# Loading sixteen tiles of y instead of four ahead of pass 2 of a two-layer convolution kernel

## The chip, the cores and the metric

The kernel runs on one core of one Trainium2 chip. The metric is the device time of one execution in microseconds. Engines: PE (TensorE), ACT (ScalarE), DVE (VectorE), POOL (GpSimd), and SP (SyncE), which here only issues DMAs. SPq marks SP's DMA issues in the rows.

## What is computed

x is 2048 x 512 channels x 8 x 8, float32. Two layers, each with a residual:

```python
x = x + L0(_gn(x))     # an 8x8 Clifford algebra product on each channel's 64 elements, plus a bias
x = x + L1(_gn(x))     # _gn: group norm of 32 groups of 16 channels
# L1(v):
h = sign(batchnorm(v, bn1))                        # statistics over batch and pixels
h = conv3x3(h, sign(conv_w) * scale, groups=16)
h = batchnorm(h, bn2) + v
return where(h > 0, h, prelu_a * h)
```

The two batch norms need statistics over the whole batch, so the work falls into three passes. Between them y (the input of L1, the normalised output of layer 0) and h (the sums of the convolution, packed as integers) go through DRAM.

## The kernel before, in words

**Pass 1** has B = 128 units of 16 images. SP loads a unit of x (2 MB) into one of the four slots of ring_x; ACT takes means and squares with ring_g as scratch (x_mean, x_square, lines 563 to 576); PE turns the unit into psT and ACT copies it to ring_gT (561); PE multiplies (product, 1024 to 1033; semaphore mixed); DVE evicts psV into ring_z (756, evicted) and counts it (765, z_counted); POOL normalises ring_z into ring_y (467, y_done); SP stores a unit of y (341). The very last unit's y is written by ACT (614, y_last) and stored by SP (370). Every x, z and y ring is therefore free at another moment.

**Between the passes** DVE, PE and POOL work out the coefficients of the first batch norm, bn1_c, in a chain of small instructions.

**Pass 2** has T2 = 256 tiles: 32 images by 128 channels, one tile for each pair of units and quarter of the channels. Tile t takes units 2(t // 4) and the next, so tiles 0 to 15 read units 0 to 7 only. For each tile:
- SP loads y in two halves of 512 KB (load_y2, 359) into slot t % 4, two slots to a unit's slot of ring_x (slots 0 and 1 of it).
- ACT takes the sign of both halves (take_sign, 624; semaphore signed) into a slot in ring_x's last quarter.
- DVE packs both into one frame (840; packed). PE runs 18 matmuls on it (1100; conv_done) into one of four PSUM regions.
- ACT converts the sums to words (unpack, 635) in word slot t % 4. It waits for PE, and from tile 4 on for the store of the word tile four before (h_stored) and its statistics (h_counted). ACT's order is: sign of t, then unpack of t - 2.
- DVE takes statistics of the words (848). SP stores them (store_h, 378), 512 KB.

All DMAs of the kernel are issued by SP in program order. In pass 2, SP's round t is: wait for the sign of t, load tile t + 4, store words t - 3. Before the rounds SP does, in this order: the store of unit 125 (in pass 1's last round), tiles 0 to 3 of y, the store of unit 126, the wait for y_last, the store of unit 127, and a wait until all of y is stored.

**Pass 3** reads y and h again (load_3, 395 and 397) and writes the output (rings y, z, g and gT hold its inputs). It begins with loads that SP puts between the last three stores of h. The change does not touch it.

Of the kernel before, what the change touches and what calls it, by code (L numbers as in the profile page):

```python
# [18 lines left out]
SIDE = 8  # L19
J = C // P  # L20
NQ = 4
# [3 lines left out]
FU = NQ * SL  # L25
UNIT = NQ * (P // GROUPS)
BANK = 512
PAIRS = GC // 2
HEAD = TAIL = 4
SLOTS = 4  # L30
# [4 lines left out]
IMG = 16  # L35
# [21 lines left out]
def two_layer_kernel(nc, x, w0, b0, conv_w, g1, be1, g2, be2, prelu_a, ident_in, quarter_in, clif_in, pick_in, route_in, out):  # L57
    N = x.shape[0]
    B = N // UNIT
    T2 = (B // 2) * J  # L60
# [15 lines left out]
    with ExitStack() as ctx:  # L76
# [3 lines left out]
        def sem(name):  # L80
            return ctx.enter_context(nc.semaphore(name))

        ring_x = sb("ring_x", [P, SLOTS, FU])
        ring_z = sb("ring_z", [P, 2, FU])
# [91 lines left out]
        def y2_slot(s):  # L176
            return ring_x[:, s // 2, 2048 * (s % 2):2048 * (s % 2) + 2048]

        def word_slot(s):
            return ring_x[:, 2, 1024 * s:1024 * s + 1024].bitcast(I32)  # L180

# [68 lines left out]
        bn1_routed = sem("bn1_routed")  # L250

        y2_loaded = [sem(f"y2_loaded{s}") for s in range(SLOTS)]
        signed = sem("signed")
        packed = sem("packed")
        conv_done = sem("conv_done")
# [25 lines left out]
        def rounds(eng, body, total, head=HEAD):  # L281

            loops = (total - head - TAIL) // SLOTS
            for c in range(head):
                body(0, c)
            with eng.Fori(0, loops) as i:
                for c in range(head, head + SLOTS):
                    body(i, c)
            for c in range(head, head + TAIL):
                body(loops, c)  # L290

        def from_round(i, c, n):

            return not (isinstance(i, int) and SLOTS * i + c < n)
# [5 lines left out]
        def row(ap, b):  # L300
            if isinstance(b, int):
                return ap[b]
            one = ap[bass.ds(b, 1)]
            return one.rearrange("a p f -> (a p) f") if len(one.shape) == 3 else one.rearrange(
                "a p n f -> (a p) n f")
# [7 lines left out]
        @block.sync  # L313
        def _(sp):
            def load_x(i, c):
                s = c % SLOTS
                sp.dma_start(ring_x[:, s, :].rearrange("p (n f) -> p n f", n=NQ), row(xb, SLOTS * i + c)).then_inc(
                    x_loaded[s], 16)

            load_x(0, 0)  # L320
            for dst, src in ((ident[:, :], ident_in), (quarter[:, :], quarter_in), (clif, clif_in),
                             (pick[:, :], pick_in), (route[:, :], route_in),
                             (cw, conv_w.rearrange("(k p) i a b -> p k (i a b)", p=P)),
                             (gb1[:, 0, :], g1.rearrange("(k p) -> p k", p=P)),
                             (gb1[:, 1, :], be1.rearrange("(k p) -> p k", p=P)),
                             (gb2[:, 0, :], g2.rearrange("(k p) -> p k", p=P)),
                             (gb2[:, 1, :], be2.rearrange("(k p) -> p k", p=P)),
                             (w0_sb[:, :], w0.rearrange("o i p -> (i p) o"))):
                sp.dma_start(dst, src, allow_slow_non_contiguous=True).then_inc(const_loaded, 16)
            sp.wait_ge(cleared, 1)  # L330
            sp.dma_start(brow[0:1, :], b0.rearrange("(a o) k -> a (o k)", a=1)).then_inc(const_loaded, 16)
            load_x(0, 1)
            for m in range(4):
                sp.dma_start(slope[GROUPS * m:GROUPS * (m + 1), :],
                             prelu_a.rearrange("(q j) -> q j", j=GC)).then_inc(const_loaded, 16)
            load_x(0, 2)

            def store_y(i, c):
                b = SLOTS * i + c
                sp.wait_ge(y_done, 4 * b + 4)  # L340
                sp.dma_start(row(y_unit, b), ring_y[:, c % 2, :]).then_inc(y_stored[c % 2], 16)

            def pass1(i, c):
                b = SLOTS * i + c
                if until(i, c, B - 3):
                    if from_round(i, c, 1):
                        sp.wait_ge(evicted, 4 * b)
                    load_x(i, c + 3)
                if from_round(i, c, 2):
                    store_y(i, c - 2)  # L350

            rounds(sp, pass1, B)

            def load_y2(i, c):

                s = c % SLOTS
                pair = 2 * (i + c // J)
                for e in range(2):
                    sp.dma_start(y2_slot(s)[:, 1024 * e:1024 * (e + 1)].rearrange("p (m f) -> p m f", m=4),  # L359
                                 row(y_chan[:, c % J], pair + e)).then_inc(y2_loaded[s], 16)  # L360

            sp.wait_ge(evicted, 4 * (B - 2))
            sp.wait_ge(y_stored[0], 16)
            sp.wait_ge(y_stored[1], 16)
            for c in range(SLOTS):
                load_y2(0, c)
            loops1 = (B - SLOTS) // SLOTS
            store_y(loops1, SLOTS - 2)
            sp.wait_ge(y_last, NQ)
            sp.dma_start(y_unit[B - 1], ring_y[:, 1, :]).then_inc(y_stored[1], 16)  # L370

            for s in range(2):
                sp.wait_ge(y_stored[s], 16 * (B // 2))

            def store_h(i, c):
                t = SLOTS * i + c
                sp.wait_ge(unpacked, t + 1)
                sp.dma_start(row(h_chan[:, c % J], i + c // J),  # L378
                             word_slot(c % SLOTS).rearrange("p (m f) -> p m f", m=4)).then_inc(h_stored[c % SLOTS], 16)

            def pass2(i, c):
                t = SLOTS * i + c
                if until(i, c, T2 - SLOTS):
                    sp.wait_ge(signed, 2 * t + 2)
                    load_y2(i, c + SLOTS)
                if from_round(i, c, 3):
                    store_h(i, c - 3)

            rounds(sp, pass2, T2, 2 * HEAD)

            def load_3(i, c):

                s = c % SLOTS
                for e in range(2):
                    sp.dma_start(y3_slot(s)[:, e].rearrange("p c f -> p (c f)"),
                                 row(y_half[:, c % 2], SLOTS * i + c // 2 * 2 + e)).then_inc(y3_loaded[s], 16)
                sp.dma_start(h3_slot(s), row(h_half[:, c % 2], 2 * i + c // 2)).then_inc(h3_loaded[s], 16)

            for s in range(SLOTS):
                sp.wait_ge(h_stored[s], 32)  # L400
            loops2 = (T2 - SLOTS) // SLOTS
            for c in range(1, SLOTS):
                store_h(loops2, c)
                load_3(0, c - 1)
            load_3(0, SLOTS - 1)
            for s in range(SLOTS):
                sp.wait_ge(h_stored[s], 16 * (T2 // SLOTS))

            def store_out(i, c):
                half = c % 2  # L410
                for e in range(2):
                    sp.dma_start(row(ob, SLOTS * i + c // 2 * 2 + e)[:, :, 512 * half:512 * half + 512],
                                 o_slot(half)[:, e]).then_inc(out_stored[half], 16)

            def pass3(i, c):
                t = SLOTS * i + c
                if from_round(i, c, 1):
                    sp.wait_ge(added, 8 * t)
                    if until(i, c, T3 - 3):
                        load_3(i, c + 3)  # L420
                    store_out(i, c - 1)

            rounds(sp, pass3, T3)
            sp.wait_ge(added, 8 * T3)
            store_out((T3 - SLOTS) // SLOTS, SLOTS - 1)
            for s in range(2):
                sp.wait_ge(out_stored[s], 16 * T3)
# [115 lines left out]
        def _(act):  # L543
# [73 lines left out]

            def take_sign(i, c):
                t, s = SLOTS * i + c, c % SLOTS
                act.wait_ge(y2_loaded[s], 32 * (i + c // SLOTS + 1))  # L620
                if from_round(i, c, 2):
                    act.wait_ge(packed, t - 1)
                for e in range(2):
                    act.activation(  # L624
                        sign_slot(c % 2)[:, e].rearrange("p (a n b) -> p n a b", a=SIDE, n=IMG),
                        y2_slot(s)[:, 1024 * e:1024 * (e + 1)].rearrange("p (n a b) -> p n a b", n=IMG, a=SIDE),
                        ACT.Sign, bias=bn1_c[:, c % J, 1:2], scale=bn1_c[:, c % J, 0:1]).then_inc(signed, 1)

            def unpack(i, c):
# [13 lines left out]
                if from_round(i, c, 2):  # L643
                    unpack(i, c - 2)

            rounds(act, pass2, T2, 2 * HEAD)
            last = (T2 - SLOTS) // SLOTS
            unpack(last, SLOTS - 2)
            unpack(last, SLOTS - 1)
# [519 lines left out]
```

## Time and profile before

| | |
|---|---|
| Median of 3 runs | 4575.77 us (4575.63 to 4576.2) |
| The profiled execution | 4573.96 us, span 4572.2 us |
| Mean granted TensorE clock in it | 0.993 |
| Busy: PE, DVE, ACT, POOL | 93%, 91%, 85%, 32% of the span |
| DMA | 1612 MB, mean 353 GB/s |
| Pass 1, between, pass 2, pass 3 | to about 1748, 1761, 2795, 4572 us |

Times in rows are microseconds from the span's start. A timeline row is start, duration, engine, line, operation, output<-inputs, shapes and count; in brackets the engine's idle time before it and what ended it. A row with a count above 1 is several instructions, merged. The duration of a DMA issue is SP's time for issuing it, not that of the transfer. PEclk is the granted TensorE clock as a share of full speed. The DMA share is the mean busy share of the core's 16 DMA engines; the profile counts it a little generously, so it can stand above 1.

### The profile page before, as it was taken

The page shows a single profiled execution, that of the slowest core. Times are in us where ns is not written, and L with a number is a line of the kernel's source. Part 1 is how long each engine was busy: PE and PEld are TensorE (multiplying, and loading weights), DVE is VectorE, ACT ScalarE, POOL GpSimd, SP SyncE. Part 2 cuts the span into 40 slices and gives each one's busy share as a digit, 9 for nine tenths or more (in the row PEclk, how much of TensorE's full clock was granted, in tenths as well). Part 3 has the DMA queues.
Part 4 walks back from the last instruction along what each step waited for, and adds up shares of the span by engine and source line. Part 5 has one row for each costly group of instructions (what it writes and reads, how often), then busy time and mean ns, then how long its engine had stood idle before and what let it go on. Part 6 is the DMA issues. An engine that isn't in the chain of part 4 may idle for free.

```text
span 4572.2 us, 82027 instructions
## 1 busy us (share of the span) xinstructions
PE 4262.5 (93%) x21700; PEld 2705.5 (59%) x21956; DVE 4171.5 (91%) x9974; ACT 3866.0 (85%) x5521; POOL 1470.4 (32%) x3476
## 2 busy tenths in 40 slices
PE   6999999999999998999999996999999999999998
PEld 6999999999999994444444443444444444444443
DVE  5999999999999998999999998999999999999998
ACT  7999999999999996888888886777777777777776
POOL 3888888888888883000000000000000000000000
PEclk9999999999999998999999998999999999999999
DMA  5888888888888889999999998999999999999998
GB/s 189 317 321 317 317 320 317 317 321 316 317 321 317 316 312 330 385 385 385 385 385 385 385 385 325 386 390 386 390 384 390 388 386 386 389 389 387 388 387 308
DMA packets 686039, 1612.17 MB, mean 353 GB/s; under 512 B 29811, under 2 KB 423795, under 8 KB 620467
## 3 DMA queue, kind: packets, MB, share of 16 engines
q1 hardware_dynamic: 686002, 1611.74, 96.0%
q8 instruction: 16, 0.26, 0.0%
q14 instruction: 21, 0.16, 0.0%
HBM read 940.55 MB, written 671.09 MB: 352 GB/s over the span
## 4 chain that ended last, share of the span: by engine, by line
PE 50%; SPq 20%; ACT 11%; DVE 9%; issue 9%; DMA 1%; DVEq 0%; ACTq 0%; POOL 0%
PE psV L1032 17%; SPq L359 12%; PE psT L1015 10%; DVE ring_x L971 8%; SPq L378 7%; PE psT L1123 5%; PE psT L1125 5%; PE psV L1125 4%; PE psV L1123 4%; PE psV L1029 3%; ACT ring_y L670 3%; ACT ring_z L670 3%; ACT ring_g L568 2%; PE psV L1119 1%; ACT late L660 1%
## 5 line engine op out<-in xcount | busy, mean ns | idle before, releaser
L1032 PE MATMUL psV<-W0T,ring_gT 128*128 128x128 f32 x8192 | 1080.4, 275 | 47.7 <-issue 34.0
L1032 PEld LDWEIGHTS psV<-W0T,ring_gT 128*128 128x128 f32 x8192 | 1077.1, 192 | 33.7
L765 DVE BATCH_NORM_STATS2 early<-ring_z 128x6 f32<-128x128 f32 x4096 | 822.6, 274 | 0.0
L756 DVE SCALAR_TENSOR_TENSOR ring_z<-psV,x_r,ring_x 128x1024 f32<-128x1024 f32 x512 | 657.3, 1284 | 118.5 <-DVE early L765 76.7
L660 ACT ACTIVATE late<-ring_x,minus_b 128x512 f32<-128x512 f32 x1024 | 639.4, 707 | 0.9 <-PE psV L1125 0.9
L848 DVE BATCH_NORM_STATS2 h_tup<-ring_x 128x6 f32<-128x512 uint16 x1024 | 630.9, 679 | 0.5
L467 POOL TENSOR_SCALAR ring_y<-ring_z,u_r,u_nm 128x1024 f32<-128x1024 f32 x508 | 601.1, 1199 | 35.6 <-POOL gn L486 35.6
L624 ACT ACTIVATE ring_x<-ring_x,bn_c 128x1024 f16<-128x1024 f32 x512 | 604.1, 1230 | 5.3 <-DVE bn_c L831 5.3
L574 ACT ACTIVATE ring_g<-ring_x,x_ms 128x1024 f32<-128x1024 f32 x512 | 585.2, 1143 | 0.0
L561 ACT ACTIVATE ring_gT<-psT 128x1024 f32<-128x1024 f32 x512 | 523.8, 1023 | 50.3 <-PE psT L1015 24.6
L1015 PE MATMUL psT<-ident,ring_x 128*128 128x128 f32 x4096 | 540.2, 275 | 4.0 <-ACT rank_lhs L580 0.4
L1100 PE MATMUL psT<-late 128*128 128x448 f16 (+3 forms) x2304 | 479.5, 363 | 62.1 <-DVE late L840 61.9
L670 ACT ACTIVATE ring_y<-ring_y,gnb 128x512 f32<-128x512 f32 x512 | 368.0, 801 | 200.0 <-DVE ring_x L971 175.8
L568 ACT ACTIVATE ring_g<-ring_x 128x1024 f32<-128x1024 f32 x512 | 536.9, 1049 | 0.0
L670 ACT ACTIVATE ring_z<-ring_z,gnb 128x512 f32<-128x512 f32 x512 | 368.1, 801 | 190.3 <-DVE ring_x L971 190.3
L1125 PE MATMUL psT<-late,early 128*128 128x512 f32 x1024 | 523.7, 593 | 0.0
L1100 PE MATMUL psV<-late 128*128 128x448 f16 (+3 forms) x2304 | 475.5, 362 | 30.9 <-DVE late L840 30.9
L989 DVE SCALAR_TENSOR_TENSOR ring_x<-ring_x,bn_q,psV 128x512 f32<-128x512 f32 x512 | 374.6, 745 | 117.7 <-PE psV L1125 90.6
L1015 PEld LDWEIGHTS psT<-ident,ring_x 128*128 128x128 f32 x4096 | 460.2, 141 | 26.4 <-ACT rank_lhs L580 26.3
L1100 PEld LDWEIGHTS psT<-late 128*128 128x128 f16 x2304 | 215.9, 98 | 324.9 <-issue 75.9
L840 DVE SCALAR_TENSOR_TENSOR late<-ring_x 128x1024 f16<-128x1024 f16 x256 | 312.8, 1222 | 97.9 <-ACT ring_x L624 89.2
L1125 PE MATMUL psV<-late,early 128*128 128x512 f32 x768 | 392.1, 592 | 0.0
(161 smaller groups left out, 5591.5 us busy)
## 6 DMA issues: line engine op xcount, KB each, us to landing
ring_x<-in_x SPq DMA_DIRECT2D x128, 2048.0 KB, 8.8
y_scratch<-ring_y SPq DMA_DIRECT2D x128, 2048.0 KB, 12.7
ring_x<-y_scratch SPq DMA_DIRECT2D x512, 512.0 KB, 7.6
out<-ring_x SPq DMA_DIRECT2D x256, 1024.0 KB, 14.5
h_scratch<-ring_x SPq DMA_DIRECT2D x256, 512.0 KB, 7.8
ring_y<-y_scratch SPq DMA_DIRECT2D x128, 1024.0 KB, 7.9
ring_z<-y_scratch SPq DMA_DIRECT2D x128, 1024.0 KB, 8.3
ring_g<-h_scratch SPq DMA_DIRECT2D x64, 1024.0 KB, 12.1
```

The costliest lines, as they stand in the source:

```text
L467: pool.tensor_scalar(ring_y[:, c % 2, :].rearrange("p (r n s) -> p n r s", r=GC, n=NQ)[:, j], ring_z[:, c % 2, SL * j:SL * (j + 1)].rearra ...
L568: act.activation(ring_g[:, 2 * (j % 2), :], ring_x[:, s, SL * j:SL * (j + 1)], ACT.Copy, scale=-1.0 / (SL * ROOT), accum_out=x_ms[:, s, 0, ...
L624: act.activation(sign_slot(c % 2)[:, e].rearrange("p (a n b) -> p n a b", a=SIDE, n=IMG), y2_slot(s)[:, 1024 * e:1024 * (e + 1)].rearrange ...
L660: act.activation(relu_slot(m), t_slot(c % 2)[:, m], ACT.Relu, bias=minus_b2[:, ch:ch + 1], scale=-1.0).then_inc(relu_done, 1)
L670: last = act.activation(v, v, ACT.Identity, bias=gnb[:, s, e, 0, n:n + 1], scale=gnb[:, s, e, 1, n:n + 1])
L756: dve.scalar_tensor_tensor(out=ring_z[:, c % 2, cols], in0=psV[:, j % 2, :], scalar=x_r[:, s, j:j + 1], in1=ring_x[:, s, cols], op0=ALU.mu ...
L765: last = dve.bn_stats(z_tup[:, s, j, 2 * r:2 * r + 2, :].rearrange("p h t -> p (h t)"), ring_z[:, c % 2, SL * j + 2 * S * r:SL * j + 2 * S ...
L848: last = dve.bn_stats(h_tup[:, c % J, c // J, q, :], parts[:, BANK * q:BANK * (q + 1)])
L1015: last = pe.transpose(psT[:, j % 2, P * r:P * (r + 1)], ring_x[:, s, SL * j + P * r:SL * j + P * (r + 1)], ident[:, :])
L1032: last = pe.matmul(psV[:, j % 2, P * r:P * (r + 1)], ring_gT[:, j, P * r:P * (r + 1)], W0T[:, :], start=False, stop=(r % 4 == 3))
L1100: last = pe.matmul(sums[:, IMG * a.start:IMG * a.stop, b.start:b.stop], conv_wT[:, c % J, tap, :], rows[:, IMG * (a.start + dy):IMG * (a.s ...
L1125: pe.matmul(sum_bank(m), diag[:, 8 * (c % 2) + m, :], relu_slot(m), start=False, stop=True).then_inc(combined, 1)
```

## The change

Tiles 4 to 15 of y get places of their own, and semaphores of their own (y2_early): tiles 4 and 5 in ring_g, 6 and 7 in ring_gT, 8 to 11 in ring_z, 12 to 15 in ring_y. SP issues their loads before pass 2's rounds, each group behind a wait for the last user of its ring. In rounds 0 to 3 SP loads tiles 16 to 19 into the slots of ring_x, in rounds 4 to 15 nothing, and from round 16 on tile t + 4 as before. The rounds of SP and ACT are unrolled for 16 tiles instead of 8.

```diff
--- before.py
+++ after.py
@@ -25,6 +25,7 @@
 FU = NQ * SL
 UNIT = NQ * (P // GROUPS)
 BANK = 512
+AHEAD = 16
 PAIRS = GC // 2
 HEAD = TAIL = 4
 SLOTS = 4
@@ -176,6 +177,16 @@
         def y2_slot(s):
             return ring_x[:, s // 2, 2048 * (s % 2):2048 * (s % 2) + 2048]
 
+        def y2_place(i, c):
+
+            if not (isinstance(i, int) and SLOTS <= SLOTS * i + c < AHEAD):
+                return y2_slot(c % SLOTS)
+            n = SLOTS * i + c - SLOTS
+            if n < SLOTS:
+                return (ring_g if n < 2 else ring_gT)[:, 2 * (n % 2):2 * (n % 2) + 2, :].rearrange("p s f -> p (s f)")
+            return (ring_z if n < 2 * SLOTS else ring_y)[:, :, :].rearrange("p s f -> p (s f)")[
+                :, 2048 * (n % SLOTS):2048 * (n % SLOTS) + 2048]
+
         def word_slot(s):
             return ring_x[:, 2, 1024 * s:1024 * s + 1024].bitcast(I32)
 
@@ -250,6 +261,7 @@
         bn1_routed = sem("bn1_routed")
 
         y2_loaded = [sem(f"y2_loaded{s}") for s in range(SLOTS)]
+        y2_early = [sem(f"y2_early{t}") for t in range(SLOTS, AHEAD)]
         signed = sem("signed")
         packed = sem("packed")
         conv_done = sem("conv_done")
@@ -353,24 +365,36 @@
 
             def load_y2(i, c):
 
-                s = c % SLOTS
+                early = isinstance(i, int) and SLOTS <= SLOTS * i + c < AHEAD
+                loaded = y2_early[SLOTS * i + c - SLOTS] if early else y2_loaded[c % SLOTS]
                 pair = 2 * (i + c // J)
                 for e in range(2):
-                    sp.dma_start(y2_slot(s)[:, 1024 * e:1024 * (e + 1)].rearrange("p (m f) -> p m f", m=4),
-                                 row(y_chan[:, c % J], pair + e)).then_inc(y2_loaded[s], 16)
+                    sp.dma_start(y2_place(i, c)[:, 1024 * e:1024 * (e + 1)].rearrange("p (m f) -> p m f", m=4),
+                                 row(y_chan[:, c % J], pair + e)).then_inc(loaded, 16)
 
             sp.wait_ge(evicted, 4 * (B - 2))
-            sp.wait_ge(y_stored[0], 16)
-            sp.wait_ge(y_stored[1], 16)
+            for s in range(2):
+                sp.wait_ge(y_stored[s], 16 * (AHEAD // J))
             for c in range(SLOTS):
                 load_y2(0, c)
             loops1 = (B - SLOTS) // SLOTS
+            sp.wait_ge(x_squared, NQ * B)
+            load_y2(1, 0)
+            load_y2(1, 1)
+            sp.wait_ge(mixed, NQ * B)
+            load_y2(1, 2)
+            load_y2(1, 3)
             store_y(loops1, SLOTS - 2)
             sp.wait_ge(y_last, NQ)
             sp.dma_start(y_unit[B - 1], ring_y[:, 1, :]).then_inc(y_stored[1], 16)
+            sp.wait_ge(z_counted, NQ * B)
+            for c in range(SLOTS):
+                load_y2(2, c)
 
             for s in range(2):
                 sp.wait_ge(y_stored[s], 16 * (B // 2))
+            for c in range(SLOTS):
+                load_y2(3, c)
 
             def store_h(i, c):
                 t = SLOTS * i + c
@@ -381,12 +405,16 @@
             def pass2(i, c):
                 t = SLOTS * i + c
                 if until(i, c, T2 - SLOTS):
-                    sp.wait_ge(signed, 2 * t + 2)
-                    load_y2(i, c + SLOTS)
+                    if not from_round(i, c, SLOTS):
+                        sp.wait_ge(signed, 2 * t + 2)
+                        load_y2(i, c + AHEAD)
+                    elif from_round(i, c, AHEAD):
+                        sp.wait_ge(signed, 2 * t + 2)
+                        load_y2(i, c + SLOTS)
                 if from_round(i, c, 3):
                     store_h(i, c - 3)
 
-            rounds(sp, pass2, T2, 2 * HEAD)
+            rounds(sp, pass2, T2, AHEAD)
 
             def load_3(i, c):
 
@@ -617,13 +645,18 @@
 
             def take_sign(i, c):
                 t, s = SLOTS * i + c, c % SLOTS
-                act.wait_ge(y2_loaded[s], 32 * (i + c // SLOTS + 1))
+                if not from_round(i, c, SLOTS):
+                    act.wait_ge(y2_loaded[s], 32)
+                elif not from_round(i, c, AHEAD):
+                    act.wait_ge(y2_early[t - SLOTS], 32)
+                else:
+                    act.wait_ge(y2_loaded[s], 32 * (i + c // SLOTS + 2 - AHEAD // SLOTS))
                 if from_round(i, c, 2):
                     act.wait_ge(packed, t - 1)
                 for e in range(2):
                     act.activation(
                         sign_slot(c % 2)[:, e].rearrange("p (a n b) -> p n a b", a=SIDE, n=IMG),
-                        y2_slot(s)[:, 1024 * e:1024 * (e + 1)].rearrange("p (n a b) -> p n a b", n=IMG, a=SIDE),
+                        y2_place(i, c)[:, 1024 * e:1024 * (e + 1)].rearrange("p (n a b) -> p n a b", n=IMG, a=SIDE),
                         ACT.Sign, bias=bn1_c[:, c % J, 1:2], scale=bn1_c[:, c % J, 0:1]).then_inc(signed, 1)
 
             def unpack(i, c):
@@ -643,7 +676,7 @@
                 if from_round(i, c, 2):
                     unpack(i, c - 2)
 
-            rounds(act, pass2, T2, 2 * HEAD)
+            rounds(act, pass2, T2, AHEAD)
             last = (T2 - SLOTS) // SLOTS
             unpack(last, SLOTS - 2)
             unpack(last, SLOTS - 1)
```

## Rows read from the trace of the kernel before

**Rows 1.** The page: span, then DMA share and GB/s in 40 slices.
```profile
span 4572.2 us, 82027 instructions
...
DMA  5888888888888889999999998999999999999998
GB/s 189 317 321 317 317 320 317 317 321 316 317 321 317 316 312 330 385 385 385 385 385 385 385 385 325 386 390 386 390 384 390 388 386 386 389 389 387 388 387 308
```

**Rows 2.** Table by stage: window, its length, each engine's busy time, PEclk, DMA share, GB/s.
```profile
0.00:1748.00 1748.00, 1640.66 (x13240) 1546.65 (x13496) 1594.99 (x5168) 1659.07 (x2702) 1455.01 (x3454) 1.00 0.85 308
1748.00:1761.00 13.00, 2.50 (x9) 2.13 (x10) 5.04 (x21) 7.69 (x8) 7.17 (x13) 0.50 0.80 335
1761.00:2795.00 1034.00, 947.23 (x4590) 431.90 (x4588) 938.38 (x1398) 833.70 (x763) 7.15 (x10) 1.00 1.09 384
```

**Rows 3.** Groups of instructions, 1900 to 2700 us: busy, mean ns, idle before and releasers.
```profile
L624 ACT ACTIVATE ring_x<-ring_x,bn_c 128x1024 f16<-128x1024 f32 x392 | 462.7, 1230 | 0.0
...
L635 ACT ACTIVATE ring_x<-psT 128x1024 int32<-128x1024 f32 x98 | 100.3, 1023 | 79.1 <-DMA h_scratch<-ring_x 73.1 <-DVE h_tup L848 6.0
```

**Rows 4.** Timeline of SP's queue, 1729 to 1755 us.
```profile
1729.60 0.33 SPq L341 DMA_DIRECT2D y_scratch<-ring_y  x1
1730.05 12.31 SPq L359 DMA_DIRECT2D ring_x<-y_scratch  x8
1742.41 1.87 SPq L341 DMA_DIRECT2D y_scratch<-ring_y  x1
1751.69 0.36 SPq L370 DMA_DIRECT2D y_scratch<-ring_y  x1
```

**Rows 5.** Timelines of ACT, PE and DVE: their last work of pass 1 on each ring.
```profile
1714.44 1.14 ACT L574 ACTIVATE ring_g<-ring_x,x_ms 128x1024 f32<-128x1024 f32 x1
...
1736.06 1.05 PE L1032 MATMUL psV<-W0T,ring_gT 128*128 128x128 f32 x8
...
1741.01 3.16 DVE L765 BATCH_NORM_STATS2 early<-ring_z 128x6 f32<-128x128 f32 x16
```

**Rows 6.** Table of shorter windows, columns as in rows 2.
```profile
1738.00:1748.00 10.00, 0.00 (x0) 0.00 (x0) 6.73 (x28) 0.97 (x1) 9.17 (x23) 0.58 1.10 353
1749.00:1757.00 8.00, 2.25 (x8) 2.00 (x8) 3.82 (x20) 2.69 (x4) 2.25 (x5) 0.50 1.01 434
1758.40:1761.60 3.20, 0.86 (x3) 0.43 (x4) 1.23 (x1) 3.20 (x4) 3.20 (x5) 0.50 0.17 46
```

**Rows 7.** Timeline of the first tiles of pass 2, 1759 to 1784 us.
```profile
1759.59 10.44 SPq L359 DMA_DIRECT2D ring_x<-y_scratch  x8
...
1760.74 8.59 PE L1100 MATMUL psT<-late 128*128 128x512 f16 x36 [5.96 <-DVE late L840]
...
1769.17 7.30 PE L1100 MATMUL psV<-late 128*128 128x512 f16 x36
...
1770.07 0.51 SPq L378 DMA_DIRECT2D h_scratch<-ring_x  x1
...
1776.31 7.30 PE L1100 MATMUL psT<-late 128*128 128x512 f16 x36
...
1780.08 1.02 ACT L635 ACTIVATE ring_x<-psT 128x1024 int32<-128x1024 f32 x1 [0.29 <-PE psT L1100]
```

**Rows 8.** Timeline of SP's queue at the load of tile 20.
```profile
1820.64 2.40 SPq L359 DMA_DIRECT2D ring_x<-y_scratch  x2
```

**Rows 9.** Landing times of lines 378 and 359; timeline at pass 2's end.
```profile
DMA to landing us min/median/max: 3.2/7.8/17.4
...
DMA to landing us min/median/max: 3.9/7.6/10.8
...
2798.37 1.06 SPq L395 DMA_DIRECT2D ring_y<-y_scratch  x2
...
2800.31 1.23 SPq L378 DMA_DIRECT2D h_scratch<-ring_x  x1
...
2817.81 0.17 DVE L958 TENSOR_SCALAR gnb<-gn 128x16 f32<-128x16 f32 x1 [2.12 <-DMA h_scratch<-ring_x]
```

## The prediction

> **What bounds the kernel now.** I read the page first, for the shape of the whole run [rows 1]: the core's 16 DMA engines show hardly any slack from slice 17 on, and some before it. A table by stage puts numbers on that [rows 2]. Pass 1 ends about 1748 and moves 308 GB/s at a DMA share of 0.85, so engines set its pace. Pass 2 moves 384 GB/s at a share of 1.09 for 1034 us, which is a full DMA system. The groups of instructions of 800 us of pass 2 show the same from the engines' side [rows 3]: 392 Sign activations, two for each tile, so 196 tiles in 800 us, 4.08 us a tile. ACT's idle time before the conversion of the sums to words (L635) was ended by the store of h, in all but 6 of 79 us in the group shown. A tile moves two halves of y, 1.049 MB, and one word tile, 0.524 MB; 1.573 MB at 385 GB/s is 4.09 us. So **pass 2 is bound by bytes**. Without that bound a tile would take 3.57 us: in the first tiles PE runs 36 matmuls, two tiles, in 7.14 us (1776.31 less 1769.17, one group's start to the next) [rows 7].
>
> Then I read SP's queue at the boundary [rows 4]. SP issues the store of unit 125 at 1729.60, tiles 0 to 3 of y behind it, the store of unit 126 at 1742.41 and that of unit 127 at 1751.69; tiles 4 to 7 begin at 1759.59 and the first store of h follows at 1770.07 [rows 7]. The windows show what the DMA does in between [rows 6]: loads of y alone go at 353 GB/s and stores of y alone at 434, both with a share above 1. Only 1758.4 to 1761.6 is nearly idle. **The end of pass 1, from 1729.6 on, has almost no free DMA time.**
>
> **The change, part by part.** (1) *Tiles 4 to 7 go into ring_g and ring_gT.* Their waits are for ACT's last square, which ends at 1716, and PE's last product, which ends about 1737; both are over when SP gets there, at 1742.4 [rows 4, 5]. So the waits cost nothing, but the eight DMAs stand in front of the store of unit 126. Nobody needs that store early: ACT's y of unit 127 waits for unit 125's.
> (2) *Tiles 8 to 11 go into ring_z* behind unit 127's store; the wait, for the last statistics (over by 1744.2 [rows 5]), is free. *Tiles 12 to 15 go into ring_y* once both y stores have landed. Eight DMAs are queued behind unit 127 by then, so the queue does not run dry.
> (3) *Tiles 16 to 19* are issued in rounds 0 to 3 of SP's pass 2, where tiles 4 to 7 were, in front of the first store of h. Rounds 4 to 15 issue stores of h alone. From round 16 on the order is as before: a load four tiles ahead, and a store three behind.
> (4) The twelve semaphores, and Sign reading other rings of the same type and shape, I cost at nothing; the instruction is the same 1.2 us one and no engine gains one.
>
> The chief cost is in what is queued ahead of the first store of h. It was four tiles; now twelve more (4.2 MB of tiles 4 to 7 before the y stores, 8.4 MB of tiles 8 to 15 after) come first. I follow the queue in its order of issue.
> - Unit 125 and tiles 0 to 3 are 6.3 MB and are through at 1748: in the before trace the 353 GB/s stretch of loads ends there [rows 6].
> - Tiles 4 to 7, 4.19 MB at 353 GB/s: 11.9 us, to 1759.9.
> - Units 126 and 127, 4.19 MB at 434 GB/s: 9.7 us, to 1769.6.
> - Tiles 8 to 19, 12.58 MB at 353 GB/s: 35.6 us, to 1805.2.
> - The first store of h, 0.52 MB, 1.2 us and about 1.5 us for the completion to arrive (its least landing time is 3.2 us, of which 1.2 are data [rows 9]): **landed at about 1808**. If the loads went at pass 2's 385 GB/s throughout, it would be 4 us sooner, at 1804.
>
> Who waits for it: ACT converts tile 4 into word slot 0, and for that the store of tile 0 must have landed. Before, that instruction began at 1780.08 with PE as its releaser [rows 7]. It will now wait until 1808, **28 us** (24 by the faster rate). Queued behind it on ACT are the Signs of tile 7 and later; DVE packs nothing without them and PE convolves nothing without the pack. All three stand still, and PE's granted clock will fall to 0.50, as it did in the gap between the passes [rows 6].
>
> What comes back: after 1808 tiles 4 to 19 are in the SBUF, and the engines go at 3.57 us a tile. But the DMA has only stores of h until the Sign of tile 16 lets SP issue tile 20. Sign of tile 7 begins at 1809; nine rounds of 3.57 are 32.1; Sign itself is 2.4; the slow clock costs 1.4 (two tiles took 8.59 us for 7.14 at the start [rows 7]), and about 2 come back because PE has emptied its queue of two tiles and starts tile 7 sooner after ACT. Sum 1842.9. Issue (0.9) and a landing on an almost empty queue (3.9, the least of the line that loads [rows 9]) put **tile 20 in the SBUF at 1847.7**. Before, its two halves were issued from 1820.64 on, the second at 1821.9 [rows 8], and landed the median 7.6 us later [rows 9], at 1829.5. From tile 20 on both kernels issue the same transfers in the same order and have 4.09 us of DMA work for each tile of 3.57 us, so both are bound by bytes and the distance stays: 18.2 us. I add 1 us for the start of the stream (1761.6, the restart before, came 2 us after its issue). **Sum: +19 us**, and +15 by the faster rate of loads.
>
> A count of idle DMA time agrees. After: 1807 to 1843 holds only the stores of tiles 4 to 12 or so, ten times 1.2 to 1.4 us, so 23 us are idle; before, 3 us at 1758.4 and about 2 more in the restart were. The difference is 18.
>
> The profiled execution took 4573.96 us, 1.8 under the median of 4575.77. Its sum is 4593; on the median **4595 us**. Against before, 0.2%, 9 us, is about what a measurement of this kernel can tell from no change.
>
> **A rule weighed.** The last store of h of pass 2, issued at 2800.31 behind loads for pass 3, took the longest of all to land, 17.4 us, and DVE waited for it until 2817.81 [rows 9]: transfers of SP land in the order in which their data is queued. The Trainium skill, DMA: Bandwidth & Descriptors, Queues, rings and completion order, says that on each DMA engine descriptors of one issuer's ring are consumed in ring order; by it the same 28 us stall follows. The same page's Rules for kernel authors advise to issue a DMA early and to wait for it late; by that rule alone the sum would be rival A's, since it counts the covered latency and not who stands behind the load.
>
> **Rivals.**
> *A, not slower: the stores of h pass the loads.* If a store of h shares the engines with the loads queued before it rather than following them, it lands in some 8 us like the median one, ACT never stops, and tiles 4 to 15 run at 3.57 instead of 4.08 us: 12 times 0.51 is 6.1 us, 4569.7 us. It decides where the landing stays below the 10 us between the store's issue and ACT's need (1770.07 to 1780.08 [rows 7]). For it: nothing but the early start of the loads. Against: 17.4 us above, and the bytes, as the DMA would still be full from 1742 on and could save only the 5 us in which it was idle.
> *B, a short stall.* The loads go faster than 353, or PE and ACT make up more after the stall, as ACT alone needs 3.38 us a tile. For each us that the DMA is idle less, one comes back. With half of it, +9 us: 4585 us. Against: PE's 3.57.
> *C, a longer one.* The loads of y slow the two y stores, the wait for unit 127 leaves a gap, or the stores of tiles 1 to 3 are late one after the other and each stops ACT again: 5 to 8 us more, 4602 us. Against: these stores follow each other at 1.2 us, ACT needs one each 3.57.
> *D, the loads are not early.* Twelve tiles are not loaded "while the first pass ends": SP's place in line lets only tiles 4 to 7 start before 1748. That is in my sum already; if SP sat still in front of them as well, the time would be C's.
>
> **How the numbers follow.** Forecast 0.80, A 0.07, B 0.07, C and D 0.06. The forecast's own range, with both rates of loads and 2 us either way, is 4589 to 4598. Nothing in A reaches 9 us of gain, so faster gets little, 0.03; within 0.2%, A's rest and half of B, 0.10; slower 0.87. The range is 4586 to 4602; it leaves out A, the lower part of B and the far end of C.
>
> **What would show it.** Right: one idle stretch of ACT of 24 to 30 us before a conversion (L635's new line) at 1780, released by the DMA of h_scratch; in the chain of waits it is the longest one; PE's clock at half in it; the first store of h issued near 1800 instead of 1770; after about 1808 a stretch of some 35 us with a low DMA share and a round each 3.6 us; then 385 GB/s again and pass 2's end some 19 us later. Pass 3's length unchanged. Wrong: no long wait for h_scratch, a first store of h that lands within 10 us, or a pass 2 that ends before 2795.

## The result and the profile after

The changed kernel takes 4595.66 us (median of 6 runs, 4594.82 to 4597.21) against 4575.70 for the kernel before (6 runs, 4574.46 to 4576.65): 20 us slower, ratio 1.0044 with a 95% interval of 1.0031 to 1.0057. The forecast was 4595.

The page of the changed kernel, span, DMA share and GB/s in 40 slices, answers to [rows 1]:

```profile
span 4594.9 us, 81949 instructions
...
DMA  5888888888888888999999998999999999999998
GB/s 189 317 324 315 317 319 319 316 316 323 313 319 321 317 304 293 360 385 385 385 385 385 385 385 324 386 386 388 388 387 385 390 387 389 387 388 387 390 384 310
```

Slices 16 and 17 moved 293 and 360 GB/s where 330 and 385 stood before, although transfers now start sooner. The other slices changed by a few GB/s at most. SP's queue at the boundary, with the columns of [rows 4], says in which order it now works:

```profile
1729.43 0.33 SPq L353 DMA_DIRECT2D y_scratch<-ring_y  x1
1729.88 12.31 SPq L372 DMA_DIRECT2D ring_x<-y_scratch  x8
1742.24 6.20 SPq L372 DMA_DIRECT2D ring_g<-y_scratch  x4
1748.48 5.71 SPq L372 DMA_DIRECT2D ring_gT<-y_scratch  x4
1754.23 1.87 SPq L353 DMA_DIRECT2D y_scratch<-ring_y  x1
1756.15 0.43 SPq L389 DMA_DIRECT2D y_scratch<-ring_y  x1
1756.62 19.83 SPq L372 DMA_DIRECT2D ring_z<-y_scratch  x8
1776.55 11.94 SPq L372 DMA_DIRECT2D ring_y<-y_scratch  x8
1788.54 12.16 SPq L372 DMA_DIRECT2D ring_x<-y_scratch  x8
1800.74 37.75 SPq L402 DMA_DIRECT2D h_scratch<-ring_x  x13
1844.12 0.99 SPq L372 DMA_DIRECT2D ring_x<-y_scratch  x2
```

The first store of h is issued at 1800.74; before, it was at 1770.07 [rows 7]. SP goes through 24 issues of loads, one after the other, in 44 us. It issues them at the speed of the transfers: the eight for ring_y take 11.94 us, which for 4.19 MB is 351 GB/s, while with little in flight an issue takes 0.4 us (tile 20, at 1844.12). So most of the delay of the first store of h is a late issue. From its issue to its landing it took this long:

```profile
DMA to landing us min/median/max: 8.3/8.3/8.3
```

That is 1809.0; before, it was issued 30.7 us sooner and took 6.4. The last load in front of it, issued at 1799.28, landed 8.5 us later, at 1807.8, just ahead of it. ACT's timeline from 1778 us:

```profile
1777.74 1.02 ACT L668 ACTIVATE ring_x<-psV 128x1024 int32<-128x1024 f32 x1 [0.29 <-PE psV L1133]
1778.66 2.36 ACT L657 ACTIVATE ring_x<-ring_gT,bn_c 128x1024 f16<-128x1024 f32 x2
1809.14 1.02 ACT L668 ACTIVATE ring_x<-psT 128x1024 int32<-128x1024 f32 x1 [28.12 <-issue]
1810.07 2.36 ACT L657 ACTIVATE ring_x<-ring_gT,bn_c 128x1024 f16<-128x1024 f32 x2
...
1841.56 2.36 ACT L657 ACTIVATE ring_x<-ring_x,bn_c 128x1024 f16<-128x1024 f32 x2
```

There is the 28 us stall, before the conversion of tile 4. The profile puts the wait down to "issue" and not to the store, so that the releaser alone would mislead here. The time at which the store landed, 1809.0, and the code name it: h_stored is the one wait of this instruction that was not long satisfied. The table of windows of the changed kernel, columns as in [rows 2]:

```profile
1780.00:1790.00 10.00, 8.41 (x43) 3.99 (x41) 4.98 (x8) 1.02 (x1) 0.00 (x0) 1.00 1.10 349
1790.00:1800.00 10.00, 0.00 (x0) 0.00 (x0) 0.00 (x0) 0.00 (x0) 0.00 (x0) 0.67 1.10 349
1800.00:1810.00 10.00, 0.00 (x0) 0.00 (x0) 0.00 (x0) 0.86 (x1) 0.00 (x0) 0.50 1.10 363
...
1812.00:1843.00 31.00, 29.26 (x139) 14.05 (x140) 30.54 (x43) 28.81 (x28) 0.00 (x0) 0.92 0.44 147
...
1900.00:2700.00 800.00, 728.84 (x3528) 330.81 (x3527) 727.74 (x1089) 642.85 (x589) 0.00 (x0) 1.00 1.09 385
```

Read from the top: the DMA is full of loads, then all engines stand still behind them, then the engines run and the DMA is more than half idle, since it has only the stores of tiles 4 to 12 to carry. After that pass 2 is what it was. SP issues the first load of pass 3 at 2817.36 us; before, it was 2795.58. Nearly the whole loss lies between 1780 and 1850 us, where the second half of tile 20 lands (1844.71 and 5.2 us, against 1821.49 and 8.0 us before: 20.4 us later).

### The profile page after: what moved, and what is told of

It is laid out like the page before. It is cut to its first block, busy times and chain, and to the rows that moved or that the text cites. A ratio compares the mean times of both kernels' runs of the same rounds, so it can differ in the third digit from the quotient of the medians.

```text
span 4594.9 us, 81949 instructions
## 1 busy us (share of the span) xinstructions
PE 4264.2 (93%) x21700; PEld 2707.0 (59%) x21956; DVE 4171.1 (91%) x9974; ACT 3866.6 (84%) x5521; POOL 1470.8 (32%) x3476
## 4 chain that ended last, share of the span: by engine, by line
PE 32%; SPq 20%; DVE 14%; issue 12%; POOL 10%; ACT 9%; DMA 1%; DVEq 1%; POOLq 0%; ACTq 0%
SPq L372 13%; DVE ring_x L1004 8%; PE psV L1065 7%; SPq L402 6%; PE psT L1156 5%; PE psT L1158 5%; PE psT L1048 4%; PE psV L1158 4%; PE psV L1156 4%; POOL ring_y L495 3%; ACT ring_y L703 3%; DVE early L798 3%; ACT ring_z L703 3%; PE psV L1062 1%; DVE ring_z L789 1%
## 5 line engine op out<-in xcount | busy, mean ns | idle before, releaser
L657 ACT ACTIVATE ring_x<-ring_x,bn_c 128x1024 f16<-128x1024 f32 x488 | 575.9, 1230 | 5.3 <-DVE bn_c L864 5.3
L1133 PEld LDWEIGHTS psV<-late 128*128 128x128 f16 x2304 | 218.5, 98 | 309.7 <-issue 63.9
```

What stands on the lines that cost most here:

```text
L1133: last = pe.matmul(sums[:, IMG * a.start:IMG * a.stop, b.start:b.stop], conv_wT[:, c % J, tap, :], rows[:, IMG * (a.start + dy):IMG * (a.s ...
```

## The experiments

The theory is: pass 2 ends when its bytes are through, and the change leaves the DMA idle because the first stores of h stand in SP's queue behind all the loads, so that ACT stops. Rivals were a fixed cost of the change (other rings to read from, more unrolled code), a cost for each tile ahead wherever it stands, the delay of the stores of y, and the bytes in flight as such.

**Fewer tiles ahead.** The change with 8 and with 12 in place of 16; the groups of loads ahead of the rounds that this makes needless are gone.

```diff
-AHEAD = 16
+AHEAD = 8
```

> Only tiles 4 to 7 are loaded ahead. Queue theory (the first store of h waits for all that SP queued before it): in front of it stand, from 1748 on, 4.2 MB of tiles 4 to 7, 4.2 MB of y and 4.2 MB of tiles 8 to 11, so it lands about 1784 and ACT stands still for some 4 us before its conversion for tile 4; against the kernel before -1 to +2 us, about 4576. Rival (a fixed cost of the change, from reading y out of other rings, more semaphores or longer unrolled code): most of the 20 us is still there, 4590 or more. Rival (every tile ahead costs the same 1.7 us): +7 us, 4583.

> Tiles 4 to 11 are loaded ahead. Queue theory: one more group of four tiles (11.9 us) in front of the first store of h than with 8, it lands about 1796, ACT stands still 16 us, and tile 16 is loaded 8 to 9 us later than before: 4584 to 4585. Rival (a fixed cost): 4590 or more. Rival (the same for each tile): +13 us, 4589.

Measured 4578.75 us with 8 (ratio 1.0008, 0.9998 to 1.0017) and 4586.08 with 12 (1.0023, 1.0013 to 1.0032), the kernel before beside them at 4575.48. ACT's conversion of tile 4, first with 8 tiles ahead, then with 12:

```profile
1786.55 1.02 ACT L663 ACTIVATE ring_x<-psT 128x1024 int32<-128x1024 f32 x1 [6.64 <-issue]
```

```profile
1796.56 1.02 ACT L666 ACTIVATE ring_x<-psT 128x1024 int32<-128x1024 f32 x1 [15.75 <-issue]
```

The stall grows 6.6, 15.8, 28.1 us, the time 3, 11, 20; the 3 us alone are not clear of no change. A fixed cost is out. With 12 the queue's count held, 16 us of stall for 16; with 8 it was 2.6 us too low. Both times came about 1 us above what was expected. The windows with 8 tiles ahead show why:

```profile
1755.00:1768.00 13.00, 8.47 (x30) 3.63 (x31) 4.30 (x6) 8.97 (x9) 11.11 (x16) 0.62 1.06 409
1768.00:1775.00 7.00, 7.00 (x37) 3.47 (x36) 5.44 (x8) 6.42 (x7) 0.00 (x0) 1.00 0.53 188
1775.00:1786.00 11.00, 11.00 (x57) 5.38 (x55) 8.88 (x13) 4.63 (x5) 0.00 (x0) 1.00 1.10 354
```

SP waits for all of y to be stored, with nothing queued behind unit 127's store, and the DMA runs dry at 1768 to 1775: at a share of 0.53 against 1.06 it lost about half of 7 us. In the change, and with 12, eight loads stand behind that store and cover the wait (with 12, 361 GB/s at 1768 to 1775). The count by tiles also misses: 7 and 13 us were expected by it, and 3 and 11 came.

**Where the loads stand.** All sixteen tiles ahead, but the loads of tiles 16 to 19 moved behind the first stores of h:

```diff
-                    if not from_round(i, c, SLOTS):
-                        sp.wait_ge(signed, 2 * t + 2)
-                        load_y2(i, c + AHEAD)
-                    elif from_round(i, c, AHEAD):
+                    if from_round(i, c, AHEAD):
                         sp.wait_ge(signed, 2 * t + 2)
                         load_y2(i, c + SLOTS)
+                    elif from_round(i, c, 8) and not from_round(i, c, 12):
+                        sp.wait_ge(signed, 2 * t + 2)
+                        load_y2(i, c + 8)
```

> All sixteen tiles are loaded as in the change, but tiles 16 to 19 are issued in SP's rounds 8 to 11 and not in rounds 0 to 3, so that they stand behind the first stores of h. Queue theory: the first store of h lands 12 us sooner, about 1797, the idle time of ACT is 16 us in place of 28, and the time is 12 us less than the change's, about 4584. Rival (the number of tiles ahead of pass 2, or the rings they lie in, costs the time, wherever the stores stand): no change, 4596.

Measured 4584.36 us (1.0019, 1.0009 to 1.0028), 11.3 less than the change, and the conversion of tile 4:

```profile
1795.86 1.02 ACT L668 ACTIVATE ring_x<-psT 128x1024 int32<-128x1024 f32 x1 [16.36 <-issue]
```

The same tiles in the same rings: only the loads of four tiles changed their place in the order. That rules out the number of tiles and the rings as the cause of these 11 us. The 9 us that are left over the kernel before go with the 16 us of stall that are left.

**The stores of y first.** The change, with the loads of tiles 4 to 7 moved behind the stores of units 126 and 127:

```diff
-            sp.wait_ge(x_squared, NQ * B)
-            load_y2(1, 0)
...
-            load_y2(1, 3)
             store_y(loops1, SLOTS - 2)
             sp.wait_ge(y_last, NQ)
             sp.dma_start(y_unit[B - 1], ring_y[:, 1, :]).then_inc(y_stored[1], 16)
+            sp.wait_ge(x_squared, NQ * B)
+            load_y2(1, 0)
...
+            load_y2(1, 3)
```

> The change, but the stores of units 126 and 127 are issued before the loads of tiles 4 to 7. Queue theory: the same bytes stand before the first store of h, in another order, so it lands at 1807 to 1810 as in the change, ACT stands still 27 to 29 us, and the time is 4595 to 4597. Rival (what costs is that two stores of y are held back by loads, and with them the wait for all of y): most of the loss goes, 4585 or less.

Measured 4597.41 us (1.0047, 1.0032 to 1.0063), with ACT idle for 28.51 us before the conversion of tile 4, at 1810.41. Here the order among what stands before the store of h made no difference clear of the noise; delayed stores of y were not the cost.

**The stores of h on another queue.** The change with every load in its place; POOL, which has nothing to do in pass 2 after its first few us [rows 2], issues the first sixteen stores of h, with semaphores of their own:

```diff
-                if from_round(i, c, 3):
+                if from_round(i, c, AHEAD + 3):
                     store_h(i, c - 3)
...
+            for c in range(AHEAD):
+                pool.wait_ge(unpacked, c + 1)
+                pool.dma_start(row(h_chan[:, c % J], c // J),
+                               word_slot(c % SLOTS).rearrange("p (m f) -> p m f", m=4)).then_inc(h_soft[c % SLOTS], 16)
```

> The change with its loads where they are, but the first sixteen stores of h are issued by POOL, on its own queue. Queue theory in the strong form (it is the place in SP's queue that holds the stores back, not the bytes in flight): the stores share the DMA engines with the loads, land in 10 us or little more, ACT stands still for under 5 us, tile 16 is signed at engine pace at about 1815 and the time is 0 to 9 us under the kernel before, 4567 to 4576. Rival (the stores are held back by the bytes in flight, whichever queue they are on): ACT stands still until about 1805, and the time is that of the change, 4596.

Measured **4570.64 us** (0.9991, 0.9981 to 1.0000; before 4575.48): 25 us less than the change, from nothing but who issues sixteen stores. The interval ends at no change, but each of the 10 runs is faster than each of the 31 of the kernel before. Its DMA issues from 1755 to 1830 us, with size and median time from issue to landing:

```profile
q1 hardware_dynamic: 16759, 20.56, 77.4%
q0 software_dynamic: 2304, 8.39, 28.7%
...
h_scratch<-ring_x POOLq DMA_DIRECT2D x16, 512.0 KB, 6.6
ring_x<-y_scratch SPq DMA_DIRECT2D x16, 512.0 KB, 11.5
ring_z<-y_scratch SPq DMA_DIRECT2D x8, 512.0 KB, 13.1
ring_y<-y_scratch SPq DMA_DIRECT2D x8, 512.0 KB, 12.3
```

and ACT's conversion of tile 4, which waits for PE again as in [rows 7]:

```profile
1779.91 1.02 ACT L676 ACTIVATE ring_x<-psT 128x1024 int32<-128x1024 f32 x1 [0.29 <-PE psT L1141]
```

The DMA stays full:

```profile
1780.00:1800.00 20.00, 20.00 (x103) 9.82 (x102) 20.00 (x29) 18.56 (x18) 4.51 (x6) 1.00 1.07 384
1800.00:1820.00 20.00, 20.00 (x103) 9.98 (x102) 19.98 (x29) 18.27 (x17) 3.76 (x5) 1.00 1.06 385
```

The stores land in 6.6 us while the loads now take 11 to 13. So what held the stores was their place in SP's order, not the bytes in flight. Most of it is the time of issue: POOL issued its first store at 1766.97, 34 us before SP came to it in the change, and the landing after it differs by less than 2 us (8.3 against a median of 6.6). The Trainium skill, DMA: Bandwidth & Descriptors, Queues, rings and completion order, has each DMA engine take turns among the queues that have work for it; the landing times, 6.6 against 11 to 13 us, agree. The same page of the Trainium skill, Issuing engines are not separate DMA queues, says that issuing from several engines only saves the sequencer's time of issue. That holds here: the bandwidth is the same, 384 to 385 GB/s from 1780 to 1820 us, and what POOL saved is the wait for SP's turn. That section of the Trainium skill calls the time usually small beside the DMA itself; here it is 34 us for the first store, since a row of loads, each issued at the speed of the transfers, stands in front of it, and the kernel is 25 us faster without it.

**One load beside each store.** The same places, and SP alone; tiles 8 to 19 are loaded in rounds 2 to 13, and the wait for all of y moves to round 6.

```diff
-            for c in range(SLOTS):
-                load_y2(2, c)
...
+                    elif 2 <= t < 14:
+                        sp.wait_ge(signed, 2 * t + 2)
...
+                        load_y2(i, c + 6)
```

> The same sixteen places, tiles 4 to 7 queued ahead as in the change, but tiles 8 to 19 one in each of SP's rounds 2 to 13 (round t loads tile t + 6), each beside one store of h; the wait for all of y moves to round 6. Queue theory: the first store of h has two tiles and the y stores in front of it and lands at 1777 to 1780, so ACT does not stand still; the DMA has no gap at 1758 to 1763, which is worth 3 to 5 us: 4571 to 4573. Rival (loading ahead costs by its number of tiles or its rings): 4590 or more.

Measured 4572.09 us (0.9992, 0.9983 to 1.0001; before 4575.84). Its windows:

```profile
1758.40:1761.60 3.20, 1.52 (x5) 0.72 (x6) 1.86 (x2) 3.20 (x4) 3.20 (x5) 0.50 1.15 439
1761.60:1811.00 49.40, 49.40 (x242) 23.80 (x240) 41.44 (x58) 40.98 (x38) 5.05 (x8) 0.96 1.07 385
1811.00:1820.00 9.00, 8.99 (x45) 4.11 (x43) 7.96 (x11) 6.81 (x7) 0.00 (x0) 1.00 1.09 385
1820.00:1830.00 10.00, 9.31 (x46) 4.42 (x47) 9.61 (x15) 10.00 (x10) 0.00 (x0) 1.00 0.95 310
```

The idle 3.2 us of [rows 6] are filled, after tile 0 no wait of ACT up to 1815 us reaches 1 us, and the gain is 3.7 us, within the 3 to 5 that were expected. The interval just reaches no change, but each of the 11 runs is faster than each of the 21 of the kernel before. At 1820 to 1830, 310 GB/s, a little DMA time is lost again.

**The idle time of pass 1 as well.** As the last, with tiles 0 to 3 issued before the store of unit 125, three tiles behind the last store of y, and a lead of nine. In the kernel before, the DMA stands still here, since SP waits for POOL's y of unit 125 and no load is queued in front of that wait:

```profile
1724.50:1729.50 5.00, 4.95 (x44) 4.89 (x44) 4.96 (x18) 1.51 (x2) 4.76 (x5) 1.00 0.00 0
```

```diff
+                if isinstance(i, int) and b == B - 1:
...
+                    for n in range(SLOTS):
+                        load_y2(0, n)
                 if from_round(i, c, 2):
                     store_y(i, c - 2)
...
+                        load_y2(i, c + 9)
```

> As the kernel with a lead of 6, and tiles 0 to 3 are issued before the store of unit 125, at about 1717, into the DMA's idle time of 1723.5 to 1729.6; tiles 8 to 10 follow the last store of y and rounds 2 to 10 load tile t + 9. Queue theory: 6 us more of idle DMA time are used, the first store of h lands at about 1777, and pass 2 keeps to the engines' 3.57 us a tile up to tile 16: 6 to 9 us under before, 4567 to 4570. Rival (bytes before the first store of h are too many after all): a stall of ACT at tile 4 and a time at or over 4576.

Measured 4570.54 us (0.9989, 0.9980 to 0.9998; before 4575.84). The gain is 5.3 us, a little under what was expected. The windows at tiles 11 to 18 show where it went:

```profile
1800.00:1811.00 11.00, 11.00 (x57) 5.43 (x56) 9.96 (x15) 9.16 (x9) 0.00 (x0) 1.00 1.07 379
1811.00:1819.00 8.00, 7.83 (x40) 3.67 (x39) 7.39 (x12) 8.00 (x9) 0.00 (x0) 1.00 0.37 125
```

The DMA has run out of places to load to: all of tiles up to 19 are in, and by the program tile 20 may only come after the Sign of tile 16. SP issued it at 1818.22.

**Both.** The early tiles 0 to 3, all sixteen tiles ahead, and the first sixteen stores of h on POOL's queue.

> All sixteen tiles ahead as in the change, the first sixteen stores of h on POOL's queue, and tiles 0 to 3 issued before the store of unit 125, into the DMA's idle 6 us at 1723.5 to 1729.6. Theory (pass 2 ends when the bytes are through, as long as no store of h is kept from landing): the DMA is full from about 1722 to the end of pass 2, and the 6 us show on top of the run with POOL's stores alone: 4564 to 4566. Rival (that run has already reached what the engines allow at 3.57 us a tile, so earlier bytes find no taker): 4570 to 4571, with a stretch of low DMA share before tile 20 is issued.

Measured **4567.49 us** (0.9982, 0.9973 to 0.9991; before 4575.74), the fastest of all, 8 us under the kernel before and 28 under the change. It is 3.2 us below the run with POOL's stores alone, which was measured in another session (3.4 if each is set against the kernel before beside it), between the 5 to 6 that were expected and the rival's nothing. Its windows have both:

```profile
1748.00:1800.00 52.00, 41.27 (x191) 20.59 (x192) 36.21 (x64) 40.49 (x38) 20.74 (x32) 0.82 1.07 384
...
1811.00:1819.00 8.00, 8.00 (x42) 3.92 (x40) 8.00 (x12) 7.42 (x8) 1.53 (x3) 1.00 0.63 214
```

The engines go at their own pace, and still the DMA waits some 3 us (0.4 of 8) for the Sign of tile 16. SP issued tile 20 at 1817.39, as that Sign ended. This points to the Sign of tile 16 as the next limit with sixteen places; a version with more places was not tried.

## Why the prediction was right

Point by point, by its own steps:

- *Pass 2 is bound by bytes.* Shown: every run moves 385 GB/s at a share of 1.09 from 1900 to 2700 us, and the runs without a stall are faster than the kernel before by no more than the DMA's idle time that they filled.
- *Parts 1 to 3, the waits.* They cost nothing, as said: SP passed them at 1742.24, 1748.48 and 1756.62 without a pause. That the wait for all of y was covered by the eight loads behind it was right and mattered: with 8 tiles ahead that cover was gone, and half of 7 us with it.
- *The count of the queue.* It put the landing at 1808, or 1804 by the rate of 385 GB/s. It came at 1809.0, and ACT's conversion began at 1809.14. The slower rate was the right one: loads alone went at 349 GB/s at 1748 to 1760 and at 1780 to 1800 (353 taken).
- *The stall.* 28 us forecast, 28.12 measured; PE ran dry at about 1788 and its granted clock fell to 0.50 (1800 to 1810).
- *What comes back.* Sign of tile 7 at 1810.07 (1809), that of tile 16 ended at 1843.9 (1842.9), tile 20 issued at 1844.12. The slow clock cost PE 1.9 us, not 1.4: tile 7's 18 matmuls took 5.44 us against 3.57. The landing of tile 20 was counted too low: its second half came at 1849.9, not at 1847.7, so that the distance was 20.4 us there and not 18.2. The 1.2 us of a later issue and 1 us of a longer landing make it up. The reading of [rows 8] was off too, the second half was issued at 1821.49 and not at 1821.9, but it took 8.0 us and landed at 1829.5 as counted.
- *The sum.* +19 forecast, +20 measured between the medians. The first load of pass 3 came 21.8 us later in the two profiled executions, whose own times differ by 22.7; the medians are the better measure of the total. Against the traces the sum is 2 to 3 us low, and that it meets the medians within 1 us is partly luck.
- *A transfer lands in the order of SP's queue.* The prediction took it from one store, at the end of pass 2, that landed after 17.4 us [rows 9]. The first store of h did land behind the load in front of it (1809.0 and 1807.8). The experiments show that the place in SP's order is the cause: the stall follows the bytes in front (8, 12, 16 tiles), follows the place of the loads of four tiles, ignores the order among them, and goes when POOL issues the stores. That last run changes the issuer and the queue together; an issuer of its own on SP's kind of queue was not tried.
- *Where the store waits.* The count needs only the bytes in front, and so it came out right wherever the store waits. Most of the wait is in front of its issue (30.7 us later than before), not behind it (8.3 us against 6.4). One sign of being wrong was badly chosen for that: "a first store of h that lands within 10 us" is what came, and what the forecast itself implies, with the issue near 1800 and the landing at 1808. The condition of rival A, a landing below 10 us after the issue, was met as well, and ACT stood still even so.
- *Rival A, the stores pass the loads,* did not come on SP's queue. On POOL's they do, and A's forecast of 6 us under before was near what that gave (4.8). *Rival B,* half a stall, and *C,* a longer one, did not come. Part of C, a gap behind unit 127's store, is real with 8 tiles ahead.
- *Not forecast:* the profile's releaser for the long wait. It was to be the DMA of h_scratch and is "issue".

## What to carry to other kernels

A prefetch is not free where the DMA is the bound: count what it puts in front of the first small transfer that an engine waits for, in bytes over the rate of that kind of transfer, and compare with the time until the wait. Look at the time of issue as well as at the landing: behind a row of large loads the issue itself comes late. Where a deep prefetch and a short ring of results share one queue, interleave them one to one, or give the short ring another queue. And where bytes are the bound, a prefetch gains at most the idle DMA time that it fills: here 3 to 5 us at the boundary and 6 us before it, of which the best version got 8.

## What the runs showed of the hardware

Two queues together did not go faster than one, 384 to 385 GB/s against 385, but they divided it: half-megabyte stores on POOL's queue landed in 6.6 us beside loads of SP that took 11 to 13. On SP's queue in the changed kernel a store of h took 8.3 us with loads in front and 2.9 us with none (each of the eight issued from 1812 to 1843 us).

With loads in front, SP's issues keep to the speed of the transfers: 1.5 us for each half-megabyte load of y at 1776 to 1800 us, against 0.4 us for those of tile 20. Of the 8.3 us of the first store of h, 2.9 are what it takes with nothing in front; the 5.4 that are left are, at 353 GB/s, an estimated 1.9 MB of loads that were issued but not yet done.

The rate depends on the mix: loads of y alone 349 to 353 GB/s, stores of y alone 434, the mix of pass 2 385, each at a share above 1. A forecast of the landing with the mix's rate was 1804, 5 us early.
